# Two more experts' weights asked for before the token exchange in a graph-attention and mixture-of-experts kernel

## The reference

```
x = x + gnn(layernorm(x), edges, W_l, W_r, att, bias, gamma, beta)
xf = layernorm(x)
logits = xf @ Wr + br                       # 64 experts
top2, idx = top_k(logits, 2); gates = softmax(top2)
for e in range(64):
    h = relu(xf @ W1[e] + b1[e])            # 256 -> 512
    y = h @ W2[e] + b2[e]                   # 512 -> 256
    out += combine[:, e] * y
x = x + out
```

## Time and profile before

| | us |
|---|---|
| median of 3 runs | 880.9 |
| lowest and highest of them | 873.68, 883.59 |
| the profiled execution's own time | 872.36 |
| its span, first to last instruction | 870.6 |
| TensorE busy | 721.0 (83%) |
| VectorE busy | 560.3 (64%) |
| GpSimd busy | 411.5 (47%) |
| ScalarE busy | 355.9 (41%) |

### The profile page before, as it was taken

One profiled execution on the slowest core, in us unless ns is written; L12 is line 12 of the kernel. 1 busy time (PEld: TensorE's weight loads), 2 busy tenths in 40 slices (PEclk: granted clock), 3 DMA queues, 4 the chain that ended last, 5 costly groups with the idle time before them and its releaser, 6 DMA issues. The chain is left out here.

```text
span 870.6 us, 14203 instructions
## 1 busy us (share of the span) xinstructions
PE 721.0 (83%) x4151; PEld 490.7 (56%) x4153; DVE 560.3 (64%) x1355; ACT 355.9 (41%) x1256; POOL 411.5 (47%) x405
## 2 busy tenths in 40 slices
PE   4844777997999889988988898998855499999995
PEld 2722444665666666666766565776544255555553
DVE  5653657886778777777876687878697333434333
ACT  1411334554455555555554464657632121121220
POOL 0566666366667656666765566710326011212121
PEclk9975798999999999999998899999955699999998
DMA  4545463344354435353534353510299899999995
GB/s 122 98 156 148 111 170 97 113 114 125 94 150 112 135 90 149 100 144 95 156 95 125 97 139 108 133 30 1 93 411 405 249 317 367 367 369 370 368 390 200
DMA packets 66875, 154.81 MB, mean 178 GB/s; under 512 B 17390, under 2 KB 30142, under 8 KB 66769
## 3 DMA queue, kind: packets, MB, share of 16 engines
q1 hardware_dynamic: 45824, 100.40, 34.2%
q0 software_dynamic: 18384, 51.06, 21.5%
q10 hardware_dynamic: 2592, 2.43, 0.9%
HBM read 138.76 MB, written 15.39 MB: 177 GB/s over the span
## 5 line engine op out<-in xcount | busy, mean ns | idle before, releaser
L131 POOL DMA_INDIRECT G<-xl_tab,srcI x324 | 344.6, 1064 | 196.0 <-issue 80.4
L783 ACT ACTIVATE L<-psE 128x264 f32<-128x264 f32 x324 | 126.4, 390 | 277.6 <-PE psE L696 200.0
L696 PE MATMUL psE<-G,ident 128*128 128x264 f32 x648 | 209.2, 406 | 0.0
L707 PE MATMUL agg<-msg,M 128*128 128x256 f32 x648 | 191.2, 395 | 6.4 <-issue 4.8
L693 PE MATMUL psE<-xr,MT 128*128 x972 | 176.9, 292 | 0.0
L854 DVE TENSOR_TENSOR L<-L,attb 128x792 f32<-128x792 f32 x108 | 105.7, 978 | 93.6 <-ACT M L784 46.5
L689 PE MATMUL psE<-identb,MT 128*128 128x128 bf16 x324 | 74.1, 229 | 81.4 <-issue 39.2
L805 ACT ACTIVATE msg<-G,A 128x64 f32<-128x64 f32 x432 | 136.8, 354 | 1.5 <-PE agg L707 1.2
L707 PEld LDWEIGHTS agg<-msg,M 128*128 128x128 f32 x648 | 118.5, 194 | 33.3 <-issue 17.4
L693 PEld LDWEIGHTS psE<-xr,MT 128*128 128x128 bf16 x972 | 88.5, 101 | 41.7 <-issue 6.0
L696 PEld LDWEIGHTS psE<-G,ident 128*128 128x128 f32 x648 | 105.5, 203 | 5.1
(11 more groups left out here) (302 smaller groups left out, 723.1 us busy)
## 6 DMA issues: line engine op xcount, KB each, us to landing
w<-in_L_ffn_W SPq DMA_DIRECT2D x120, 512.0 KB
relb<-rel_d SPq DMA_DIRECT2D x36, 288.0 KB
G<-xl_tab,srcI POOLq DMA_INDIRECT x324
tabs<-tab_d SPq DMA_DIRECT2D x48, 98.2 KB
X<-xs_d SPq DMA_DIRECT2D x58, 64.5 KB
xn<-in_L_ffn_W SPq DMA_DIRECT2D x6, 512.0 KB
h_in<-in_L_ffn_W SPq DMA_DIRECT2D x6, 512.0 KB
xs_d<-zslot SPq DMA_DIRECT2D x8, 322.5 KB
```

Source lines behind the costliest of these rows:

```text
L131: nc.gpsimd.indirect_dma_start(out=G[:, g % RG, u * DX:(u + 1) * DX], out_offset=None, in_=xl_tab, in_offset=bass.IndirectOffsetOnAxis(ap= ...
L696: nc.tensor.matmul(psE[:, e, 0:DX], ident[:, :], G[:, s % RG, u * DX:(u + 1) * DX], start=False, stop=True).then_inc(expanded, 1)
L707: last = nc.tensor.matmul(agg[:, bass.ds(w * D, D)], M[:, s % RM, u * P:(u + 1) * P], msg[:, s % RA, u * D:(u + 1) * D], start=False, stop ...
L783: nc.scalar.activation(L[s % RL][:, u * DX:(u + 1) * DX], psE[:, e, 0:DX], ACT.Relu)
```

## The change

SyncE loads 19 experts in the route phase in place of 17. The last of them, number 18, goes into the space of `xn`, and so SyncE waits for the sixth lift ahead of it. After `moved` only expert 19 is left to be loaded by the loop over `range(FIRST, 2 * RP)`.

```diff
-RP, FIRST = RING // 2 + 1, 17
+RP, FIRST = RING // 2 + 1, RING + 1
...
             for e in range(FIRST):
+                if e == RING:
+                    sp.wait_ge(lifted, NG)
                 load_first(sp, W1, w1, w1_in, e // 2, e % 2, e)
                 load_second(sp, W2, w2, w2_in, e // 2, e % 2, e)
```

## The result

The changed kernel is slower, by about 1% or less. Over 20 runs of each its median is 881.12 us against 877.92, +3.2 us or +0.36%; the ratio is 1.0075, with a 95% interval of 1.0044 to 1.0105. The ratio is formed from the faster runs of each kernel alone, which are cut off from the lowest run of each, so it need not be the quotient of the medians. The profiled execution took 883.25 us, with a span of 881.5.

A forecast was written before the change was run, and what follows sets the result against it. TensorE was taken to bound the expert phase to about 843 us, weights only the last pairs, behind a head of scatter and token loads. Tail -0.9, scatter +1.4, place 1 -1.1 gave -0.6: 880.9 to 880.3 us, range 873 to 886.5.

The forecast's parts named there:

- Its own sign of being wrong: Expert phase's head: first product over 3 us earlier or later than 12.0 us after the last scatter's issue would mean contention.
- The wait for the lifts costs nothing: Route phase, SyncE: lifts are over at 631.4 us, the new wait is reached at about 664, so no cost.
- four DMAs flow in the gap: Before the expert phase: 2.1 MB of weights, 5.2 us of transfer, fill the 676 to 681 us gap, ending about 682.4.
- the steady pairs keep 4.95 us: Expert phase, TensorE: pairs follow one another at TensorE's own 4.95 us, as before the change.
- the clock rises as before: TensorE at the expert phase's start: its granted clock rises as long after the start as before, so 0.
- The last scatter, +1.4: Head: weights of experts 17 and 18 beside GpSimd's last scatter delay it by 0 to 2.9 us; the middle, +1.4, taken.
- The tokens of place 1, -1.1: Head: place 1's token loads meet 4 us of weight transfers in place of 7.7; 0 to -2.9 us, -1.1 taken.
- The tail, -0.9: Last pairs: an earlier weight stream removes most of the 1.2 us TensorE waits for weights; -0.2 to -1.2, -0.9 taken.
- 0.88 each: SyncE's 16 token loads before the second round: 14.13 us read as 0.88 each; at 0.53, over 5.6 us sooner.
- The one on the other side: Head: weights delay scatter and place 0 by 2.9 us each, less 1.2 at the tail; +4.6, 885.5 us, chance 0.19.
- The gap was worth its whole length: Expert phase bound by the DMA stream: filling the gap brings 5 us, 875.3 us; 0.03 for 5 us or more.
- the dip: DMA share at 696 to 699 us, 0.27, put down to the full ring; fetching sooner only makes it longer.

The follow-up runs named there:

- after_junk: The changed kernel with 2 MB more weights queued behind expert 18, into a table nothing reads; executed once for its trace: scatter 6.29 us, head 20.12, route to end 254.40.
- before_again: The kernel before, executed again with nothing changed; ratio 1.0015 (0.9966 to 1.0064).
- after_x1sp: The changed kernel with the tokens of place 1 loaded by SyncE right behind its wait for `moved`, in place of ScalarE; ratio 1.0063 (1.002 to 1.0106).

## Why the prediction was right or wrong

The forecast was 880.3 us, within 1% of before; the time is 881.12 and the change of 0.44 to 1.05% lies about within what I called the same. The direction is wrong: -0.6 us was forecast, and the ratio's whole interval lies above 1. That 880.3 and 881.12 lie so close is luck: the forecast was built on a median of 880.9, and over 20 runs the kernel before has 877.92. Its own sign of being wrong came true as well: TensorE's first product comes 16.2 us after the last scatter (14.8 and 15.9 in the repeats), where over 3 us more than 12.0 was to mean that contention is the account.

- *The wait for the lifts costs nothing; four DMAs flow in the gap; the steady pairs keep 4.95 us; the clock rises as before.* Right: no pause at `xn`, share 1.01 in the former gap, bodies of 163.4 to 164.1. The head's first products took 3.35 us at the clock's lower level, 3.58 before, and the granted clock rose from 0.50 to 1.00 at 703.2 and 691.8 us, 2.9 and 3.4 us after the first product began.
- *The last scatter, +1.4.* Mis-sized: +2.5 (2.0 to 3.1 against the mean of before). The middle of 0 and 2.9 had nothing to speak for it; after_junk shows a price that doesn't grow with the queue, and the end of 2.9 was near it.
- *The tokens of place 1, -1.1.* This step failed, in sign. It measured +1.0. I counted bytes (4 us of transfers in place of 7.7) and left the order of issue alone. In the kernel before SyncE waited 1.2 us longer than ScalarE, for VectorE's table. I named that slack in the scatter's term ("SyncE itself moves less") and didn't draw the consequence: with `moved` later than the table, both open together, the place 0 loads lose their free road (3.9 becomes 7.5 to 7.8, and place 1 comes 1.1 to 1.5 behind), and expert 19's 1 MB beside them costs 7.80 - 4.15 = 3.7 us, which is no less than what 3 MB cost in the kernel before (7.64 to 8.05).
- *The tail, -0.9.* Too large. The wait at the last `second` is gone, but before_again's body is 163.52, so that the 1.2 us of the first trace were mostly that execution's. It measured -0.2. The stream did come sooner, 4.1 to 4.7 us behind the first product in place of 10.4 and 10.6, but the "0.88 each" that the working drew from 16 loads in 14.13 us is a misreading: the 12 loads took 0.67 each, and 2.9 us of the 14.13 lie between them and the last four.
- *The rivals.* The one on the other side had the mechanism: weights in front of the scatter and of place 0. Its scatter (2.9) and place 0 (6.8, measured 7.5 to 7.8) were near, but it had place 1 follow at 4.0 us, where it follows at 1.1 to 1.5, so its 885.5 is too high. "The gap was worth its whole length" (by its own sum 875.9, not 875.3) is refuted as a gain: the dip came, and the body fell by 0.2. A part of it is true that I had given nothing: the second round starts 6 us sooner, which would let a shorter head count (after_x1sp), and it is bought for more than it brings.
- *Spread.* A trace of one execution carries a figure of the head to about 1.5 us (14.8 to 16.2 in three of one kernel), and the time of one execution to 10 us. The sum of small terms, 0.6, was within that, and all three had errors larger than it: 1.1, 2.1 and 0.7.

## What to carry to other kernels

A gap in the DMA share ahead of a phase change may be what the last small, latency-bound transfers need: look at what waits for the transfers that land in it before filling it with bulk. When a step on the chain moves later, compare it with every other wait that opened behind it; two issues kept apart by 1 us of slack may now start together. And where a stream and an engine are both full, time saved at the head of the one is paid at the tail of the other, until both are moved.

## What the runs showed of the hardware

- The last scatter, 98 rows of 1032 bytes 1.3 us behind another of 98, takes 5.2 to 6.6 us with weights moving beside it all the while, and 3.2 to 4.0 where their last rows start 2.1 to 2.9 us after it (5.1 once, where the last started at 4.1 us). With 1, 2 and 4 MB queued it was 5.2, 5.5 to 6.6 and 6.3.
- Two token loads of place 0 and two of place 1, 66 KB each, are usable after 4.15 us alone and after 7.8 with 1 MB of weights issued at the same instant, more than the 2.6 us that this MB takes at 406 GB/s. The first row of the loads then moves 2.6 to 2.8 us after their issue, in place of 1.3.
- SyncE needs some 8 us to issue 12 token loads in a row, 0.65 to 0.67 us each (8.06 us in the kernel before, 7.86 in the changed one). With four register loads and four more token loads it is 13 to 14 us, so what is issued ahead of the weights costs more than its bytes.
